# Macaron block: the attention's token sum once per sequence in the projection's bank, added to x1 by GpSimd, identity by a scaled x1

## The chip, the core and the metric

The kernel runs on one core of one Trainium2 chip. The metric is the device time in microseconds, the median of three runs. The engines are TensorE (PE; its weight loads are PEld), VectorE (DVE), ScalarE (ACT), GpSimd (POOL) and SyncE (SP), which issues every DMA. Each works through its own instruction queue in order, and they meet only through semaphores.

## The reference, cut to what matters

There are 32 sequences of 512 tokens with 256 values each, and three residual stages per sequence:

```
x = x + 0.5 * ffn(layernorm(x))      # x1
x = x + attn(layernorm(x))           # x2
x = x + 0.5 * ffn(layernorm(x))      # x3

attn(x):  a = softmax(q k^T / 16)          # 512 x 512
          a = eye + a
          a = a - mean(a, axis=-1)
          return a @ x
ffn(x):   fp4 quantise x;  g = x Wg^T, u = x Wu^T;  h = silu(g) * u
          fp4 quantise h;  return h Wd^T
```

A row of the softmax sums to 1, so a row of `eye + a` sums to 2 and its mean is 2/512. Subtracting the mean therefore subtracts 2/512 times the sum of all the tokens, the same for every row, and the identity adds the token itself. So with n = layernorm(x1), x2 = x1 + n + softmax @ n - (2/512) * sum over tokens of n.

## The kernel before, in words

The work is cut into **tiles** of 128 tokens: four tiles per sequence for the first feed-forward stage and four for the second, 256 tiles in all. Time is cut into **slots**; eight slots (j = 0 to 7) make one **iteration**, and each slot starts one tile. Slots 0 to 3 of an iteration start the first stage's tiles of sequence `it`, slots 4 to 7 the second stage's tiles of sequence `it - 2`. Besides a tile, a slot may start one of three other items: a `query` (half of a sequence's attention, two token tiles; slots 0 and 2), a `front` (layernorm and quantisation of one sequence for a feed-forward stage; slots 0 and 4), and an `afront` (layernorm and projection for the attention; slot 6). An item's steps are spread over later slots by **age**: `s.tile[2]` is the tile that was started two slots ago.

Every engine has a function `emit(s, pair)` that lists its steps of one slot in a fixed order written out by hand; `walk` runs it over the slots (two iterations form the body of a hardware loop). What one engine's slot 5 does at the same time as another's slot 5 is settled by the semaphores alone: an engine may run ahead or behind by a slot or more.

The steps of a tile n and who does them, with lines of the profile: gate and up products in three column cuts into `gu_ps` (PE, L1163 `products`); `silu` of the gate half (ACT, L851); `hid` = up * silu (DVE, L959); block maxima, scale and reciprocal `h_am`, `h_s`, `h_rs` (DVE, L971, L1014, L1045, L1076); division by the block scale `h_xq` (POOL, L586); `h_unit`, `h_sigma`, `h_sh` (ACT, L676, L679, L701); lifting `h_y` (ACT, L706); rounding `h_t`, `h_q` (DVE, L1033, L1063); dequantised halves `h_dq` (DVE, L1082 and L980); transposition `hT` by DMA (SP); the down product into `out_ps` (PE, L1264); the residual addition (DVE, L990). A gate/up product of tile n + 1 waits until ACT and DVE have read tile n out of `gu_ps`, which exists once.

The steps of an `afront`: sums, means and squares of x1 (ACT, L714, L789, L804, L831), `a_ve`, `a_rstd`, `a_shift` (POOL, L571, L599, L604), the normalised tokens `a_xs` (ACT, L796, L823), their f16 halves `xs_hi` (ACT, L845) and `xs_lo` (POOL, L593), transposition to `aT` (SP), two projections into the one bank `tr_a` (PE), read out by ACT (L818, L663). The bank's users take it in turns that are counted in `A_TURNS`; `OUT_TURNS` counts the turns of the two banks of `out_ps`.

The steps of a `query`: two score products, softmax with `s_nmax` (DVE, L941) and two exponentials (ACT, L720, L738), p in two f16 halves, `pT` by DMA, and two `attend` products into `out_ps`, each added to x1 by DVE (L1069, L951) to give x2. One `attend` is 20 matmuls of 256 columns: 12 for softmax @ n, and 8 for the identity and the mean, where a constant 128 x 128 matrix (`own_sp` for the tile's own tokens, `other_sp` for the others) multiplies the halves of all four token tiles.

The exponential and the silu use different function tables of ScalarE, so each pair of exponentials costs two table loads.

Of the kernel before, what the change touches and what calls it, by code (L numbers as in the profile page):

```python
# [159 lines left out]
def macaron_kernel(nc, x_in, wq_in, bq_in, wk_in, bk_in, wg_in, wu_in, wd_in, out):  # L160
    slots, info = schedule()
    turn_q0, turn_q1, turn_down, turn_att0, turn_att1 = (
        info[k] for k in ("q0", "q1", "down", "att0", "att1"))
    TPP, QPP, FPP, SPP = 2 * SLOTS, 2 * QPS, 4, 2
    TURNS_A = 2 * SPP
# [5 lines left out]
    with ctx:  # L171
# [36 lines left out]
        own_sp = sb("own_sp", [P, P], F16)  # L208
# [51 lines left out]
        a_shift = sb("a_shift", [P, TILES])  # L260
        a_xs = sb("a_xs", [P, TILES, D])
        xs_hi = sb("xs_hi", [P, TILES, D], F16)
# [24 lines left out]
        w_rs = sb("w_rs", [P, WCOLS // FP4_BLOCK])  # L287
# [80 lines left out]
        a_xs_done = sig("a_xs_done", 2 * TILES)  # L368
        xs_lo_done = sig("xs_lo_done", 2)
# [82 lines left out]
        def out_bank(turn):  # L452
            return out_ps[:, turn % 2, 0:D]
# [5 lines left out]
        def _(sp):  # L459
# [42 lines left out]
            def emit(s, pair):  # L502
                if s.front[1] is not None:
                    f = s.front[1]
                    sp.wait_ge(f_dl_done.sem, f_dl_done.at(f + 1, pair))
                    sp.sem_inc(sp_passed.sem, 1)
                    if pair is not None or f >= 2:
                        sp.wait_ge(gu_full.sem, gu_full.at(3 * TILES * (f - 1), pair))
                        sp.sem_inc(sp_passed.sem, 1)
                    sp.dma_start_transpose(xT[:, f % 2, :, :, :, :].rearrange("p h t c k -> p (h t c) k"),  # L510
                                           f_dq[:, :, :].rearrange("p h d -> p (h d)")).then_inc(xT_in[f % 2].sem, 16)
                if s.afront[0] is not None:
                    turn_tokens(s.afront[0], 0, pair)
                if s.query[2] is not None:
                    turn_probs(s.query[2], 0, pair)
                if s.j == 0 and 1 <= s.it + 1 < SEQS:
                    b = s.it + 1
                    at = b if pair is None else pair * 2 + b
                    if b >= 2:
                        last = [n for n, (ffn, seq, t) in enumerate(info["tile"]) if (ffn, seq, t) == (1, b - 2, TILES - 1)][0]  # L520
                        sp.wait_ge(out_added.sem, out_added.at(turn_down[last] + 1, pair))
                    sp.dma_start(x0[:, b % 2, :, :], x_view[at] if pair is None else
                                 x_view[bass.ds(at, 1)].rearrange("s p t d -> (s p) t d")).then_inc(x_loaded[b % 2].sem, 16)
                if s.query[2] is not None:
                    turn_probs(s.query[2], 1, pair)
                if s.afront[0] is not None:
                    turn_tokens(s.afront[0], 1, pair)
                if s.tile[0] is not None:
# [6 lines left out]
                    sp.dma_start_transpose(hT[:, n % 2, :, :], h_dq[:, n % 2, :]).then_inc(hT_in[n % 2].sem, 16)  # L535
                if s.j == 3 and 0 <= s.it - 3 < SEQS:
# [3 lines left out]
                    sp.wait_ge(out_added.sem, out_added.at(turn_down[last] + 1, pair))  # L540
                    sp.dma_start(out_view[at] if pair is None else
                                 out_view[bass.ds(at, 1)].rearrange("s p t d -> (s p) t d"),
                                 x3[:, b % 2, :, :]).then_inc(stored[b % 2].sem, 16)

# [6 lines left out]
        def _(pool):  # L551
            g = nc.gpsimd

            def emit(s, pair):
                if s.front[2] is not None:
                    f = s.front[2]
                    pool.wait_ge(f_ss_done.sem, f_ss_done.at(TILES * (f + 1), pair))
                    pool.sem_inc(pool_passed.sem, 1)
                    g.tensor_scalar(f_ve[:, :], f_ss[:, :], 1.0 / D, EPS, ALU.mult, ALU.add).then_inc(f_ve_done.sem, 1)
                if s.front[3] is not None:  # L560
                    f = s.front[3]
# [774 lines left out]
```

## Time and profile before

| | us |
|---|---|
| median of three runs (2389.05 to 2400.36) | 2394.25 |
| the profiled execution, its own time | 2397.43 |
| the span of the profiled execution | 2395.6 |
| PE busy (matmuls, ends modelled) | 2099.0 (88%) |
| DVE busy | 2069.8 (86%) |
| ACT busy | 1674.6 (70%) |
| POOL busy | 750.7 (31%) |
| mean granted TensorE clock | 0.969 of 2.4 GHz |

The first 73 us of the span load and quantise the weights and bring up the first tile; about 216 to 2240 us is the steady state, in which all items overlap; the last 150 us drain the pipeline. Busy times in the profile run from start to end of an instruction, and neighbours on one engine overlap by some tens of nanoseconds, so the distance from one start to the next (called pitch in the prediction) is a little shorter than the duration that is listed.

### The profile page before, as it was taken

The page shows a single profiled execution, that of the slowest core. Times are in us where ns is not written, and L with a number is a line of the kernel's source. Part 1 is how long each engine was busy: PE and PEld are TensorE (multiplying, and loading weights), DVE is VectorE, ACT ScalarE, POOL GpSimd, SP SyncE. Part 2 cuts the span into 40 slices and gives each one's busy share as a digit, 9 for nine tenths or more (in the row PEclk, how much of TensorE's full clock was granted, in tenths as well). Part 3 has the DMA queues.
Part 4 walks back from the last instruction along what each step waited for, and adds up shares of the span by engine and source line. Part 5 has one row for each costly group of instructions (what it writes and reads, how often), then busy time and mean ns, then how long its engine had stood idle before and what let it go on. Part 6 is the DMA issues. An engine that isn't in the chain of part 4 may idle for free. (4 is left out here: it accounts for less than half of the span.)

```text
span 2395.6 us, 46422 instructions
## 1 busy us (share of the span) xinstructions
PE 2099.0 (88%) x13514; PEld 1249.1 (52%) x13514; DVE 2069.8 (86%) x3961; ACT 1674.6 (70%) x4315; POOL 750.7 (31%) x664
## 2 busy tenths in 40 slices
PE   2678999999999998999989999898999999899875
PEld 1344555555555555555555555555555555555442
DVE  6567998999989898998999899898989989899764
ACT  3357777777777777777777777786777778777641
POOL 3122333332333333233333332333333233333211
PEclk9879999999999999999999999999999999999887
DMA  1233554554445445444544544445454444544432
GB/s 55 42 69 72 93 104 82 101 100 94 95 87 104 94 97 96 95 96 81 109 93 91 96 101 99 91 91 104 91 95 101 95 89 88 103 95 87 90 57 57
DMA packets 741596, 214.25 MB, mean 89 GB/s; under 512 B 706464, under 2 KB 741152, under 8 KB 741408
## 3 DMA queue, kind: packets, MB, share of 16 engines
q1 hardware_dynamic: 741408, 212.54, 45.1%
q14 instruction: 167, 1.37, 0.2%
q8 instruction: 21, 0.34, 0.1%
HBM read 19.53 MB, written 16.78 MB: 15 GB/s over the span
## 5 line engine op out<-in xcount | busy, mean ns | idle before, releaser
L1163 PE MATMUL gu_ps<-wgu_hi,xT 128*128 128x512 f16 (+1 forms) x3072 | 956.9, 366 | 64.5 <-DMA xT<-f_dq 55.0
L586 POOL TENSOR_TENSOR tile_area<-tile_area,h_rs 128x704 f32<-128x704 f32 x256 | 390.3, 1525 | 1291.1 <-DVE h_rs L1076 1291.1
L1163 PE MATMUL gu_ps<-wgu_lo,xT 128*128 128x512 f16 (+1 forms) x1536 | 562.5, 366 | 0.0
L1163 PEld LDWEIGHTS gu_ps<-wgu_hi,xT 128*128 128x128 f16 x3072 | 303.6, 99 | 377.0 <-issue 63.2
L1264 PE MATMUL out_ps<-wd_hi,hT 128*128 128x256 f16 x1536 | 364.0, 280 | 134.8 <-DMA hT<-h_dq 134.8
L1264 PE MATMUL out_ps<-wd_lo,hT 128*128 128x256 f16 (+1 forms) x1536 | 378.4, 281 | 0.0
L959 DVE SCALAR_TENSOR_TENSOR tile_area<-gu_ps,gu_unit,tile_area 128x704 f32<-128x704 f32 x256 | 241.5, 944 | 130.1 <-PE gu_ps L1163 63.7
L851 ACT ACTIVATE tile_area<-gu_ps,gu_unit 128x704 f32<-128x704 f32 x256 | 215.5, 842 | 188.8 <-PE gu_ps L1163 188.4
L706 ACT ACTIVATE h_y<-tile_area 128x704 bf16<-128x704 f32 x256 | 200.3, 782 | 92.2 <-POOL tile_area L586 92.2
L1264 PEld LDWEIGHTS out_ps<-wd_hi,hT 128*128 128x128 f16 x1536 | 153.4, 100 | 203.0 <-issue 120.3
L971 DVE TENSOR_REDUCE h_am<-tile_area 128x44 f32<-128x704 f32 x256 | 227.1, 887 | 6.7
L1033 DVE SCALAR_TENSOR_TENSOR tile_area<-h_y,tile_area 128x704 f32<-128x704 bf16 x256 | 226.4, 885 | 4.8 <-ACT h_y L706 4.8
L1063 DVE SCALAR_TENSOR_TENSOR h_q<-h_y,tile_area 128x704 f16<-128x704 bf16 x256 | 227.5, 889 | 0.2
L1163 PEld LDWEIGHTS gu_ps<-wgu_lo,xT 128*128 128x128 f16 x1536 | 152.0, 99 | 125.1 <-issue 7.1
L1264 PEld LDWEIGHTS out_ps<-wd_lo,hT 128*128 128x128 f16 (+1 forms) x1536 | 151.9, 99 | 82.4 <-issue 57.0
L1163 PE MATMUL out_ps<-xs_hi,pT 128*128 128x256 f16 x1024 | 191.0, 275 | 3.0 <-DMA pT<-p 3.0
L1264 PE MATMUL out_ps<-wd_late,hT 128*128 128x256 f16 x1280 | 192.5, 283 | 0.0
L676 ACT ACTIVATE h_unit<-h_rs 128x1 f32<-128x1 f32 x256 | 49.8, 195 | 179.4 <-DVE h_rs L1076 175.9
L1163 PE MATMUL sc_ps<-aT,qT_hi 128*128 128x512 f16 x512 | 154.0, 383 | 2.4 <-DVE p L999 1.2
L565 POOL TENSOR_TENSOR f_xq<-f_xn,f_rs 128x1024 f32<-128x1024 f32 x64 | 124.0, 1937 | 93.1 <-DVE f_rs L937 93.1
L980 DVE TENSOR_TENSOR h_dq<-h_q,h_sl 128x704 f16<-128x704 f16 x256 | 144.2, 563 | 0.0
L1163 PE MATMUL out_ps<-xs_lo,pT 128*128 128x256 f16 x512 | 140.8, 275 | 0.0
(169 smaller groups left out, 4090.7 us busy)
## 6 DMA issues: line engine op xcount, KB each, us to landing
x<-in_L_attn_x SPq DMA_DIRECT2D x32, 512.0 KB, 3.9
out<-x_later SPq DMA_DIRECT2D x32, 512.0 KB, 3.6
hT<-h_dq SPq DMA_TRANSPOSE x256, 3.6
pT<-p SPq DMA_TRANSPOSE x128, 3.2
xT<-f_dq SPq DMA_TRANSPOSE x64, 4.3
w_raw<-in_L_ffn_w_down SPq DMA_DIRECT2D x1, 704.0 KB, 7.5
w_raw<-in_L_ffn_w_gate SPq DMA_DIRECT2D x1, 640.0 KB, 4.6
w_raw<-in_L_ffn_w_up SPq DMA_DIRECT2D x1, 640.0 KB, 5.7
```

The lines of the kernel that those rows point to most:

```text
L565: g.tensor_tensor(blocks(f_xq[:, :], XB), blocks(f_xn[:, :], XB), per_block(f_rs[:, :], XB), ALU.mult).then_inc(f_xq_done.sem, 1)
L586: g.tensor_tensor(blocks(h_xq[:, n % 2, :], FB), blocks(hid[:, n % 2, :], FB), per_block(h_rs[:, n % 2, 0:FB], FB), ALU.mult).then_inc(xq_ ...
L676: a_.activation(h_unit[:, n % 2:n % 2 + 1], h_rs[:, n % 2, FB:FB + 1], ACT.Copy, scale=-SH).then_inc(unit_done.sem, 1)
L706: a_.activation(h_y[:, n % 2, :], h_xq[:, n % 2, :], ACT.Abs, scale=LIFT).then_inc(lifted.sem, 1)
L851: a_.activation(sg[:, n % 2, :], gu_ps[:, 0:FF], ACT.Silu, scale=gu_unit[:, :]).then_inc(silu_done.sem, 1)
L959: v.scalar_tensor_tensor(out=hid[:, n % 2, :], in0=gu_ps[:, FF:GU], scalar=gu_unit[:, :], in1=sg[:, n % 2, :], op0=ALU.mult, op1=ALU.mult) ...
L971: v.tensor_reduce(h_am[:, n % 2, 0:FB], blocks(hid[:, n % 2, :], FB), AX.X, ALU.max, apply_absolute_value=True).then_inc(am_done.sem, 1)
L980: v.tensor_tensor(pairs(h_dq[:, n % 2, FF:2 * FF]), pairs(h_q[:, n % 2, :]), per_pair(h_sl[:, n % 2, :, :], FB), ALU.mult).then_inc(dl_don ...
L1033: v.scalar_tensor_tensor(out=h_t[:, n % 2, :], in0=h_y[:, n % 2, :], scalar=ROUND_MIN, in1=h_xq[:, n % 2, :], op0=ALU.max, op1=ALU.add).th ...
L1063: v.scalar_tensor_tensor(out=h_q[:, n % 2, :], in0=h_y[:, n % 2, :], scalar=ROUND_MIN, in1=h_t[:, n % 2, :], op0=ALU.max, op1=ALU.subtract ...
L1163: ins = t_.matmul(dst, x, y, start=(i == 0), stop=(i == len(todo) - 1))
L1264: ins = t_.matmul(out_bank(turn_down[n]), h, w, start=(i == 0), stop=(i == len(terms) - 1))
```

## The change

1. `attend` keeps its 12 matmuls of softmax @ n; the 8 matmuls with constants are gone, and so is `own_sp`. A new product `add_tokens`, once per sequence, forms the same 8 products with `other_sp` (minus 2/512 times the sum of the tokens) in the bank `tr_a`, as a third turn after the two projections.
2. ScalarE reads that out to `token_sum` (128 x 256), and scales x1 in place, tile by tile: x1 = x1 * (1 + a_rstd / SX) + a_shift / SX, which is x1 + n. The factors `a_own` come from two small GpSimd instructions.
3. GpSimd adds `token_sum` to the four tiles of x1 in one instruction of 128 x 1024 values.
4. VectorE's two additions that give x2 are the same instructions; each waits for `x1_ready` (and for the previous reader of x2) as well.
5. The order of the steps of a slot is written anew on all five queues, and most steps are one or two slots older. The tile's steps, before to after: first two cuts of gate/up on PE 0 to 1, third cut 0 to 2, silu 0 to 2, `hid` and block maxima 0 to 1, the rest up to `h_rs` 0 to 2, GpSimd's `h_xq` 2 to 3, ScalarE's `h_sh`, `h_y` 2 to 4, rounding 1 to 3, low half of `h_dq` 2 to 3, down product 3 to 5, addition 3 to 5; SyncE's `hT` stays at 0. A query's scores go from 2 to 3 (first) and 4 (second), its exponentials from 3 to 5, its attends from 5 to 6 and 7. The projections go from age 3 to 4 and 5, the token sum has age 6. On SyncE the transposition of a `front` goes from the head of the slot's list to behind `hT`, and the two of an `afront` go together ahead of the query's.
6. `w_rs` lies in `a_xs` during the setup (memory only). Waits on `out_added` for two tiles take the later of two turns.

The diff, cut to its core, in the order turns, TensorE, GpSimd, ScalarE, VectorE. The ScalarE step that is shown for t = 0, 1 stands a second time, for t = 2, 3, at `afront[7]`; the VectorE step stands at `query[6]` and `query[7]`.

```diff
-A_TURNS = (("q0", "afront", 3), ("q1", "afront", 3))
-OUT_TURNS = (("att0", "query", 5), ("att1", "query", 5), ("down", "tile", 3))
+A_TURNS = (("q1", "afront", 5), ("sum", "afront", 6), ("q0", "afront", 4))
+OUT_TURNS = (("down", "tile", 5), ("att0", "query", 6), ("att1", "query", 7))
...
             def attend(a, i, turn):
-                t = 2 * (a % QPS) + i
                 return products(out_bank(turn), [(pT[:, i, 0, k, :], pT[:, i, 1, k, :], xs_hi[:, k, :], xs_lo[:, k, :])
-                                                 for k in range(TILES)],
-                                [((own_sp if k == t else other_sp)[:, :], xs[:, k, :])
-                                 for k in range(TILES) for xs in (xs_hi, xs_lo)])
+                                                 for k in range(TILES)])
+            def add_tokens():
+                return products(tr_a[:, 0:D], [], [(other_sp[:, :], xs[:, k, :]) for k in range(TILES) for xs in (xs_hi, xs_lo)])
...
+                if s.afront[6] is not None:
+                    b = s.afront[6]
+                    pe.wait_ge(xs_hi_done.sem, xs_hi_done.at(b + 1, pair))
+                    pe.wait_ge(xs_lo_done.sem, xs_lo_done.at(b + 1, pair))
+                    if pair is not None or turn_sum[b] >= 1:
+                        pe.wait_ge(a_free.sem, a_free.at(turn_sum[b], pair))
+                    add_tokens().then_inc(a_full.sem, 1)
...
+                    g.tensor_scalar(a_own[:, 0:TILES], a_rstd[:, :], 1.0 / SX, 1.0, ALU.mult, ALU.add).then_inc(a_own_done.sem, 1)
+                    g.tensor_scalar(a_own[:, TILES:2 * TILES], a_shift[:, :], 1.0 / SX, 0.0, ALU.mult, ALU.add).then_inc(a_own_done.sem, 1)
+                    pool.wait_ge(xs_hi_done.sem, xs_hi_done.at(b + 1, pair))
...
+                    g.tensor_tensor(xs_lo[:, :, :], a_xs[:, :, :], xs_hi[:, :, :], ALU.subtract).then_inc(xs_lo_done.sem, 1)
...
-                if s.tile[2] is not None:
-                    n = s.tile[2]
+                if s.tile[3] is not None:
+                    n = s.tile[3]
                     pool.wait_ge(rs_done.sem, rs_done.at(n + 1, pair))
...
+                if s.afront[7] is not None:
+                    b = s.afront[7]
+                    pool.wait_ge(a_free.sem, a_free.at(turn_sum[b] + 1, pair))
+                    pool.wait_ge(x1_own_done.sem, x1_own_done.at(TILES * (b + 1), pair))
+                    g.tensor_tensor(x1[:, b % 2, :, :], x1[:, b % 2, :, :],
+                                    token_sum[:, :].unsqueeze(1).broadcast_to([P, TILES, D]), ALU.add).then_inc(x1_ready.sem, 1)
...
+                if s.afront[5] is not None:
+                    b = s.afront[5]
+                    act.wait_ge(a_own_done.sem, a_own_done.at(2 * b + 2, pair))
+                    act.wait_ge(a_xs_done.sem, a_xs_done.at(TILES * b + 2, pair))
+                    for t in (0, 1):
+                        a_.activation(x1[:, b % 2, t, :], x1[:, b % 2, t, :], ACT.Identity, scale=a_own[:, t:t + 1],
+                                      bias=a_own[:, TILES + t:TILES + t + 1]).then_inc(x1_own_done.sem, 1)
...
+                if s.afront[7] is not None:
+                    b = s.afront[7]
+                    act.wait_ge(a_full.sem, a_full.at(turn_sum[b] + 1, pair))
+                    if pair is not None or b >= 1:
+                        act.wait_ge(x1_ready.sem, x1_ready.at(b, pair))
+                    a_.activation(token_sum[:, :], tr_a[:, 0:D], ACT.Copy, scale=1.0 / (SP * SX)).then_inc(a_free.sem, 1)
...
                     dve.wait_ge(out_full.sem, out_full.at(turn_att1[a] + 1, pair))
+                    dve.wait_ge(x1_ready.sem, x1_ready.at(seq + 1, pair))
+                    if pair is not None or seq >= 2:
+                        dve.wait_ge(f_xn_done.sem, f_xn_done.at(TILES * (front_of[(2, seq)] + 1 - FPP), pair))
                     v.scalar_tensor_tensor(out=x2[:, seq % 2, t, :], in0=out_bank(turn_att1[a]), scalar=1.0 / (SP * SX),
                                            in1=x1[:, seq % 2, t, :], op0=ALU.mult, op1=ALU.add).then_inc(out_added.sem, 1)
```

After the change the order of a tile's steps in VectorE's slot is: addition (age 5), `h_am` total (2), `h_t` and `h_sl` (3), `h_q` (3), `h_s` (2), high `h_dq` (3), `h_rs` (2), low `h_dq` (3), `hid` (1), block maxima (1). ScalarE's slot 2 reads, in order: `h_unit`, `h_sigma`, `h_sh`, `h_y` (age 4), `a_xs` (four), `xs_hi`, sums of a front's tiles 2 and 3, their mean, squares of its tiles 0 and 1, silu (age 2). GpSimd's slot 2 reads: `a_rstd`, `a_shift`, `a_own` (two), `xs_lo`, `h_xq`; `a_ve` is the last step of its slot 1.

## Rows read from the trace of the kernel before

**Rows 1.** Busy (count) PE, PEld, DVE, ACT, POOL; clock, DMA share, GB/s.

```profile
1201.00:1547.00 346.00, 317.54 (x2097) 190.17 (x2096) 315.74 (x609) 258.16 (x670) 113.80 (x101) 1.00 0.48 95
```

**Rows 2.** Timeline of VectorE (start us, us): one step, twice, four iterations apart.

```profile
1237.00 1.03 DVE L976 TENSOR_TENSOR qT_lo<-qT,qT_hi 128x512 f16<-128x512 f32 x1
...
1513.71 1.03 DVE L976 TENSOR_TENSOR qT_lo<-qT,qT_hi 128x512 f16<-128x512 f32 x1
```

**Rows 3.** Waits of VectorE, same stretch: us, times, longest; largest and last.

```profile
DVE tile_area L959 <- ACT tile_area L851: 10.3, 6, 2.7
DVE tile_area L959 <- PE gu_ps L1163: 3.6, 5, 0.7
...
DVE x_later L990 <- PE out_ps L1264: 0.8, 1, 0.8
```

**Rows 4.** Waits of TensorE in the same stretch, the two largest.

```profile
PE out_ps L1264 <- DMA hT<-h_dq: 15.4, 13, 2.3
PE tr_a L1163 <- DMA aT<-xs_lo: 8.6, 5, 2.1
```

**Rows 5.** Timeline of VectorE: a slot with tile work alone, and the next `hid`.

```profile
1218.09 0.95 DVE L959 SCALAR_TENSOR_TENSOR tile_area<-gu_ps,gu_unit,tile_area 128x704 f32<-128x704 f32 x1
...
1227.15 0.95 DVE L959 SCALAR_TENSOR_TENSOR tile_area<-gu_ps,gu_unit,tile_area 128x704 f32<-128x704 f32 x1 [2.58 <-ACT tile_area L851]
```

**Rows 6.** Timeline of ScalarE in the same slot, ahead of that late `hid`.

```profile
1220.85 0.20 ACT L697 ACTIVATE f_nm<-f_sum 128x2 f32<-128x2 f32 x1 [1.86 <-issue]
...
1221.90 0.40 ACT L751 ACTIVATE f_scrap<-x_later 128x256 f16<-128x256 f32 x1
...
1222.69 1.07 ACT L796 ACTIVATE a_xs<-x_later,a_shift,a_rstd 128x256 f32<-128x256 f32 x2
...
1224.87 1.06 ACT L845 ACTIVATE xs_hi<-a_xs 128x1024 f16<-128x1024 f32 x1
1225.83 0.83 ACT L851 ACTIVATE tile_area<-gu_ps,gu_unit 128x704 f32<-128x704 f32 x1
1226.56 0.49 ACT L866 ACTIVATE f_scrap<-x_later,f_nm 128x256 f16<-128x256 f32 x1
...
1227.54 0.49 ACT L872 ACTIVATE f_scrap<-x_later,f_nm 128x256 f16<-128x256 f32 x1
```

**Rows 7.** Timeline of TensorE: an attend's first matmul, and the one behind its 20th.

```profile
1214.73 0.27 PE L1163 MATMUL out_ps<-xs_hi,pT 128*128 128x256 f16 x1
...
1216.91 0.33 PE L1163 MATMUL gu_ps<-wgu_hi,xT 128*128 128x384 f16 x1
```

**Rows 8.** Instruction groups by form over the span: busy us, mean ns.

```profile
L796 ACT ACTIVATE a_xs<-x_later,a_shift,a_rstd 128x256 f32<-128x256 f32 x64 | 34.5, 586 | 1.8 <-POOL a_shift L604 1.8
...
L892 ACT ACTIVATE wd_late<-sc_ps,w_scale 128x256 f16<-128x256 f32 x2 | 0.9, 466 | 0.0
...
L980 DVE TENSOR_TENSOR h_dq<-h_q,h_sl 128x704 f16<-128x704 f16 x256 | 144.2, 563 | 0.0
...
L565 POOL TENSOR_TENSOR f_xq<-f_xn,f_rs 128x1024 f32<-128x1024 f32 x64 | 124.0, 1937 | 93.1 <-DVE f_rs L937 93.1
```

**Rows 9.** Timeline of GpSimd: a tile's `h_xq` and the attention's norm.

```profile
1217.59 1.45 POOL L586 TENSOR_TENSOR tile_area<-tile_area,h_rs 128x704 f32<-128x704 f32 x1 [0.77 <-DVE h_rs L1076]
...
1220.24 0.21 POOL L604 TENSOR_TENSOR a_shift<-a_nm,a_rstd 128x4 f32<-128x4 f32 x1 [0.23 <-POOL a_rstd L599]
```

**Rows 10.** Timelines of GpSimd and VectorE: `xs_lo`, and an `h_dq` that starts under it.

```profile
1294.77 2.13 POOL L593 TENSOR_TENSOR xs_lo<-a_xs,xs_hi 128x1024 f16<-128x1024 f32 x1
...
1296.40 0.88 DVE L980 TENSOR_TENSOR h_dq<-h_q,h_sl 128x704 f16<-128x704 f16 x1
```

**Rows 11.** Timelines of GpSimd and TensorE at the head: last weights, first two tiles.

```profile
53.50 1.49 POOL L632 TENSOR_TENSOR w_raw<-tile_area,w_s 128x768 f32<-128x768 f32 x1 [3.42 <-DVE tile_area L1118]
...
67.33 0.59 PE L1163 MATMUL gu_ps<-wgu_hi,xT 128*128 128x512 f16 x1 [17.27 <-DMA xT<-f_dq]
...
79.81 0.58 PE L1163 MATMUL gu_ps<-wgu_hi,xT 128*128 128x512 f16 x1 [0.66 <-issue]
```

More of the change, by code:

```diff
@@ L717, in emit @@
+                if s.query[5] is not None:
+                    a = s.query[5]
                     act.wait_ge(bias_done.sem, bias_done.at(a + 1, pair))
@@ L760, in emit @@
+                if s.front[3] is not None:
+                    f = s.front[3]
                     ffn, seq = info["front"][f]
@@ L984, in emit @@
+                if s.tile[5] is not None:
+                    n = s.tile[5]
                     ffn, seq, t = info["tile"][n]
@@ new lines, in emit @@
+                if s.tile[3] is not None:
+                    n = s.tile[3]
+                    dve.wait_ge(lifted.sem, lifted.at(n + 1, pair))
+                    v.scalar_tensor_tensor(out=h_t[:, n % 2, :], in0=h_y[:, n % 2, :], scalar=ROUND_MIN,
+                                           in1=h_xq[:, n % 2, :], op0=ALU.max, op1=ALU.add).then_inc(t_done.sem, 1)
+                    dve.wait_ge(sh_done.sem, sh_done.at(n + 1, pair))
+                    v.scalar_tensor_tensor(out=h_sl[:, n % 2, :, :], in0=twice(h_s[:, n % 2, 0:FB], FB),
+                                           scalar=h_unit[:, n % 2:n % 2 + 1], in1=h_sh[:, n % 2, :, :],
+                                           op0=ALU.mult, op1=ALU.subtract).then_inc(sl_done.sem, 1)
@@ new lines, in emit @@
+                if s.front[3] is not None:
+                    f = s.front[3]
+                    dve.wait_ge(f_lifted.sem, f_lifted.at(f + 1, pair))
+                    v.scalar_tensor_tensor(out=f_t[:, :], in0=f_y[:, :], scalar=ROUND_MIN, in1=f_xq[:, :],
+                                           op0=ALU.max, op1=ALU.add).then_inc(f_t_done.sem, 1)
+                if s.tile[3] is not None:
+                    n = s.tile[3]
+                    dve.wait_ge(t_done.sem, t_done.at(n + 1, pair))
+                    v.scalar_tensor_tensor(out=h_q[:, n % 2, :], in0=h_y[:, n % 2, :], scalar=ROUND_MIN,
+                                           in1=h_t[:, n % 2, :], op0=ALU.max, op1=ALU.subtract).then_inc(q_done.sem, 1)
@@ L995, in emit @@
+                if s.query[4] is not None:
+                    a = s.query[4]
                     dve.wait_ge(scale_done.sem, scale_done.at(a + 1, pair))
@@ L1071, in emit @@
[L1071 to L1083 removed]
+                    dve.wait_ge(hid_done.sem, hid_done.at(n + 1, pair))
```

841 lines of the change are left out of this document (415 added, 426 removed).

## The prediction

> **What bounds the kernel now.** I read first the busy table of a steady stretch, then the waits of the two busiest engines there, then the timelines around the longest wait. In the stretch of 346.0 us TensorE is busy for 317.5 us, VectorE for 315.7, ScalarE for 258.2 and GpSimd for 113.8 [rows 1]: two engines at 91 to 92% and none full. The stretch holds five iterations, since a step that occurs once per iteration lies (1513.71 - 1237.00) / 4 = 69.2 us apart [rows 2]. VectorE's waits come in nine rows of together 26.6 us, of which the first two and the last are shown [rows 3], 5.3 per iteration, so its work alone is 69.2 - 5.3 = 63.9 us. TensorE's come in four rows of together 28.3 us, of which the two largest are shown [rows 4], 5.7 per iteration, all but 0.7 of the 28.3 for a DMA; its work is 63.5 us. Either engine would allow an iteration of about 64 us, and the other 5 us are a matter of who waits for whom.
>
> VectorE is the end that counts, because the longest waits sit there: `hid` behind the silu, 10.3 of the 26.6 us [rows 3]. The timeline shows one. VectorE starts `hid` of a slot that holds tile work and one attention addition alone at 1218.09 and has nothing left 6.5 us later; the next `hid` comes 2.58 us late, released by ScalarE [rows 5]. ScalarE meanwhile had sat 1.86 us at a step for which the profile names no releaser, and then went through sums, `a_xs`, `xs_hi` before the silu at 1225.83 [rows 6]. So the worst wait is ScalarE's list in a light slot of VectorE, not a matmul.
>
> **Part 1, the matmuls that go.** An attend of 20 matmuls takes 1216.91 - 1214.73 = 2.18 us, 0.109 each [rows 7]. A sequence has four attends; 32 constant matmuls go and 8 come back, so TensorE loses 24 x 0.109 = 2.6 us per iteration, 84 us in all, and has 60.9 us of work left. VectorE loses nothing: its two additions stay. Its 63.9 us are therefore the floor of the iteration, and the removed matmuls are worth at most the 5.3 us of waits, and only those that TensorE causes.
>
> **Part 2, the work that comes.** ScalarE gets four scalings of x1, the form of `a_xs` at 0.586 us, and one read of 128 x 256 from PSUM, 0.47 by `wd_late` [rows 8]: 2.8 us per iteration at most, 54.4 in place of 51.6. GpSimd gets two small instructions of about the 0.21 us of `a_shift` [rows 9] and the addition of 1024 columns, between `f_xq`'s 1.94 [rows 8] and `xs_lo`'s 2.13 [rows 10]: 2.4 to 2.6 us on an engine that is a third busy. None is a bound by its sum; what counts is whom they hold up. The scalings wait for `a_own` and for `a_xs`, both a slot old. GpSimd's addition stands behind `h_xq` in its slot 5, and VectorE's first reader behind `h_rs` in its slot 6, about 8 us later for 2 us of work, so `x1_ready` costs nothing; were it late, low `h_dq` and `hid` would stand behind it. TensorE's token sum waits for ScalarE's second projection read, with the next gate/up queued behind, but that waits for a silu that comes later in ScalarE's list anyway. On SyncE `xT` goes behind `hT` and the two `aT` ahead of `pT`; the low `h_dq` that starts `hT` now stands ahead of `hid` in VectorE's list instead of behind the block maxima, some 2 us earlier, and this covers most of the hT wait of 15.4 / 5 = 3.1 us per iteration [rows 4].
>
> **Part 3, the order.** I follow the new lists of all engines through one iteration with the starts of the timelines, from VectorE's `h_rs` in slot 0 until that step comes round again. Most slots close without a wait, because TensorE's load is now even: before, slots 5 and 7 carried two attends each, 4.4 us on top of a tile; after, slots 6, 7, 0 and 1 carry one each of 12 x 0.109 = 1.3 us, and TensorE's work per slot is 60.9 / 8 = 7.6 us on average against VectorE's 8.0. Waits appear in five places.
> Slot 1: `hid` needs the silu at the end of ScalarE's slot 2. From `h_rs` the chain is: `h_xq` to `a_shift` end 1220.45 - 1217.59 = 2.9 us [rows 9], with `a_ve` between them now, 0.4 more, 3.3; four `a_xs` 1224.87 - 1222.69 = 2.2; `xs_hi` 1.0; sums of two tiles 1222.69 - 1221.90 = 0.8; their mean 0.2; two squares 1227.54 - 1226.56 = 1.0; silu 0.7 to 0.8 [rows 6]: together 9.3 us. VectorE gets from `h_rs` to this `hid` in one light slot, 6.5 us [rows 5], and one low `h_dq`, 0.4 net of overlap: 6.9. Wait 2.4 us.
> Slot 0: the silu stands behind x1's sums and squares, which wait for the addition: 0.3. Slot 2: `h_xq` stands behind `xs_lo`, which waits for `xs_hi`, so `h_t` comes 0.2 late, and `f_xn` comes 0.3 late. Slot 3: the addition behind the projection, 0.2.
> Sum 3.4 us. The iteration becomes 63.9 + 3.4 = 67.3, which is 1.9 less. The gap of 1.86 us in ScalarE [rows 6] then falls into a slot 0 in which the silu is ready some 3.5 us before VectorE asks for it, by the same walk.
>
> A cost from both sides: GpSimd's new addition may slow a VectorE step beside it. The low `h_dq` takes 0.88 us under `xs_lo` [rows 10] against 0.56 on average [rows 8]; one such meeting per iteration costs 0.3 us, none costs 0, and no row speaks for a gain. I take 0, since the VectorE steps that stand beside the addition are not the two halves of `h_dq`; 0.3 x 29 = 9 us more stay in the range.
> The Trainium skill (Perfetto Trace Analysis, Optimizing Scalar/DVE Operations) says that GpSimd and VectorE share a read port, so that moving work between them might not help. By that rule the iteration would be 67.6 in place of 67.3; the row of 0.88 us agrees in kind.
>
> **Head and tail.** At the head the first layernorm's GpSimd steps move behind the last weight unit, which ends at 54.99 [rows 11]; I put the first gate/up 5 us later than 67.33. But TensorE's remaining weight transposes, which lie between the first tile and the second at 79.81 [rows 11], now come ahead of the first tile, while it would wait anyway. Net -2 us, within 6 either way. The tail has the same chain from the last `hid` to the store: 0, within 6.
>
> **Sum.** The steady state, 216 to 2240 us, holds 29 iterations: 29 x 1.9 = 55 us, and 2 at the head. The profiled execution took 2397.4 us, so it becomes 2340; it stood 3.2 above the median 2394.25, so I predict 2337 us. Its own bounds: waits of 2.0 to 4.7 us per iteration give 2298 to 2375.
>
> **Rivals.**
> *Waits nearly vanish* (0.2). If ScalarE reaches its slot 2 earlier than I have it, the 2.4 us go and the waits are 0 to 1.5 us: 29 x 3.8 to 5.3 gives 2238 to 2282. For it: TensorE and the DMAs have slack everywhere. Against: `h_unit` pins ScalarE's list to `h_rs`.
> *No gain* (0.14). VectorE's work is what it was, and waits of 5.3 us come back in other places: 2392. For it: the longest wait of before was ScalarE's, and ScalarE gets more work.
> The Trainium skill (Perfetto Trace Analysis, Identifying the Most-Contended Engine) says that matmul busy time misleads because matmuls are pipelined, and that for VectorE occupancy is a fair measure. By that rule VectorE is the bound and the change does not relieve it; the waits above say that it is not full.
> *ScalarE becomes the pacemaker, slower* (0.12). The scalings stand ahead of `h_y` in slot 5 and ahead of `f_xn` in slot 3, the token sum ahead of a silu. If all 2.7 us land in front of VectorE, the iteration is 67.3 + 2.7 = 70.0: 29 x 0.8 = 23 us more, 2415. It decides from 1.9 us on. For it: table loads share slot 5. Against: I find `hid` in slots 3 to 5 ready 1 us or more ahead of VectorE.
> *TensorE's clock falls, the change brings less work but not less time* (0.04). It was granted 1.00 in the stretch [rows 1] with waits of up to 2.3 us [rows 4]; I see one idle of 2.8 us in slot 2. If one tile's gate/up ran at 1.2 instead of 2.4 GHz, 3.5 us more, the 6.4 us of TensorE's room would take it; two would bring back 2390.
>
> **Chances.** Forecast 0.5, rivals 0.2, 0.14, 0.12, 0.04. About 0.5% (12 us) is what a measurement of this kernel can tell from no change. Faster: the forecast but for its upper edge and the first rival, 0.70. Same: 0.17. Slower: 0.13. The range that leaves out 2 in 10 reaches from 2250, inside the first rival, to 2404, short of the slower one.
>
> **What would show it.** In the profile after: attends of 12 matmuls, 1.3 us; VectorE busy as before, its waits down to some 3.4 us per iteration with the largest still `hid` behind the silu, in the slot in which ScalarE does `a_xs`; TensorE's wait for hT mostly gone; `x1_ready` in no row of waits; an iteration of 67.3 us. Wrong if `hid` waits for TensorE, if VectorE's longest wait is for a scaling or `x1_ready`, or if its work per iteration is not 63.9 us.

## The result and the profile after

The changed kernel takes 2376.1 us (median of 6 runs, 2369.2 to 2380.0) against 2395.0 for the kernel before: a ratio of 0.992, with a 95% interval of 0.990 to 0.994. That is 0.8% faster; forecast were 2337 us, 2.4%. The profiled execution took 2375.2 us with a span of 2372.8.

The busy row of the same stretch of 346 us after the change, columns as in [rows 1]:

```profile
1200.00:1546.00 346.00, 312.52 (x1955) 181.22 (x1956) 323.92 (x604) 269.85 (x692) 125.86 (x115) 0.96 0.48 95
```

VectorE is busy for 323.9 us instead of 315.7, ScalarE for 269.9 instead of 258.2, and TensorE's granted clock is no longer 1.00. VectorE's timeline with the step that [rows 2] show, in four of its five places:

```profile
1228.66 0.68 DVE L984 TENSOR_TENSOR qT_lo<-qT,qT_hi 128x512 f16<-128x512 f32 x1
...
1295.57 0.68 DVE L984 TENSOR_TENSOR qT_lo<-qT,qT_hi 128x512 f16<-128x512 f32 x1
...
1367.76 0.68 DVE L984 TENSOR_TENSOR qT_lo<-qT,qT_hi 128x512 f16<-128x512 f32 x1
...
1508.47 0.68 DVE L984 TENSOR_TENSOR qT_lo<-qT,qT_hi 128x512 f16<-128x512 f32 x1
```

Four iterations take 279.8 us, 70.0 each, no less than the 69.2 of before. But they alternate: 66.9 us, then 72.2 (over the whole loop 67.5 and 72.0 on average). From the first such step to the last of the 32 the two kernels take 2134.5 and 2133.8 us, so the steady state gained nothing; 6.1 us of the 22.8 in the spans lie ahead of it and 16.0 behind it.

VectorE's waits in the stretch (us, times, longest), the answer to [rows 3], and two of TensorE's, the answer to [rows 4]:

```profile
DVE f_dq L961 <- issue: 9.3, 3, 3.2
DVE s_nmax L1087 <- PE sc_ps L1205: 5.3, 3, 1.8
DVE f_am L1073 <- ACT f_xn L831: 1.4, 5, 0.3
DVE tile_area L1111 <- ACT tile_area L908: 0.8, 5, 0.2
DVE p L1119 <- ACT p L685: 0.5, 2, 0.3
```

```profile
PE sc_ps L1205 <- ACT rho L894: 7.5, 5, 1.5
...
PE out_ps L1259 <- DMA hT<-h_dq: 1.0, 2, 0.5
```

The wait of `hid` for the silu is gone (0.8 after 10.3), and so is TensorE's for hT (1.0 after 15.4). In their place stand a gap of 3 us for which the profile names no releaser, and a wait for the scores. The gap lies in the longer iterations; the wait lies in these and in one of the shorter, the one from 1367.76, which takes 68.6 us. The timelines of VectorE and TensorE where one begins, and the busy row of the 5 us behind it:

```profile
1200.13 0.89 DVE L1124 TENSOR_REDUCE h_am<-tile_area 128x44 f32<-128x704 f32 x1
1204.20 0.69 DVE L961 TENSOR_TENSOR f_dq<-f_q,f_sh 128x1024 f16<-128x1024 f16 x1 [3.19 <-issue]
```

```profile
1205.94 0.40 PE L1259 MATMUL out_ps<-wd_hi,hT 128*128 128x256 f16 x1 [3.35 <-DVE x_later L974]
1206.13 0.42 PE L1259 MATMUL out_ps<-wd_lo,hT 128*128 128x256 f16 x1
```

```profile
1206.00:1211.00 5.00, 5.00 (x23) 3.18 (x24) 4.97 (x9) 4.87 (x18) 1.77 (x3) 0.50 0.56 105
```

`f_dq` is the first step in the body of VectorE's loop, and the gap occurs 13 times over the span, once between two runs of the loop's body, which is gone through 14 times: VectorE stands while the loop turns. TensorE, which needs a buffer of out_ps from it, idles 3.35 us, and in the 5 us behind that its granted clock is 0.50, the lower of its two levels (1.2 GHz): one matmul of 256 columns follows the other after 0.21 us instead of 0.11.

### The profile page after: what moved, and what is told of

The parts are those of the page before. It is cut to its first block, busy times and chain, and to the rows that moved or that the text cites. A ratio compares the mean times of both kernels' runs of the same rounds, so it can differ in the third digit from the quotient of the medians.

```text
span 2372.8 us, 45698 instructions
## 1 busy us (share of the span) xinstructions
PE 2049.9 (86%) x12746; PEld 1184.7 (50%) x12746; DVE 2135.3 (90%) x3961; ACT 1752.3 (74%) x4475; POOL 831.4 (35%) x759
## 4 chain that ended last, share of the span: by engine, by line
issue 60%; POOL 15%; DVE 10%; ACT 10%; PE 3%; DMA 1%; POOLq 1%; DVEq 0%; ACTq 0%; SPq 0%
POOL tile_area L612 6%; POOL x_later L618 3%; POOL f_rstd L589 2%; POOL a_rstd L564 1%; ACT a_xs L755 1%; DVE tile_area L1009 1%; ACT xs_hi L793 1%; ACT a_xs L774 1%; PE out_ps L1259 1%; PE gu_ps L1205 1%; DVE f_t L1018 1%; DVE tile_area L1111 1%; ACT L908 1%; ACT L762 1%; ACT f_xn L785 1%
## 5 line engine op out<-in xcount | busy, mean ns | idle before, releaser
L1205 PE MATMUL gu_ps<-wgu_hi,xT 128*128 128x512 f16 (+1 forms) x3072 | 929.4, 364 | 87.1 <-ACT tile_area L908 41.6
L612 POOL TENSOR_TENSOR tile_area<-tile_area,h_rs 128x704 f32<-128x704 f32 x256 | 381.9, 1492 | 1229.9 <-DVE h_rs L1060 1229.9
L1259 PE MATMUL out_ps<-wd_hi,hT 128*128 128x256 f16 x1536 | 370.2, 283 | 86.8 <-DMA hT<-h_dq 45.0
L1259 PE MATMUL out_ps<-wd_lo,hT 128*128 128x256 f16 (+1 forms) x1536 | 384.4, 284 | 0.0
L1205 PE MATMUL sc_ps<-aT,qT_hi 128*128 128x512 f16 x512 | 172.2, 421 | 47.7 <-ACT rho L894 43.0
L1078 DVE TENSOR_TENSOR h_dq<-h_q,h_sl 128x704 f16<-128x704 f16 x256 | 213.3, 833 | 0.0
L1205 PE MATMUL out_ps<-xs_hi,pT 128*128 128x256 f16 x1024 | 197.5, 281 | 9.6 <-DVE x_later L1068 8.8
```

What stands on the lines that cost most here:

```text
L612: g.tensor_tensor(blocks(h_xq[:, n % 2, :], FB), blocks(hid[:, n % 2, :], FB), per_block(h_rs[:, n % 2, 0:FB], FB), ALU.mult).then_inc(xq_ ...
L1078: v.tensor_tensor(pairs(h_dq[:, n % 2, FF:2 * FF]), pairs(h_q[:, n % 2, :]), per_pair(h_sl[:, n % 2, :, :], FB), ALU.mult).then_inc(dl_don ...
L1205: ins = t_.matmul(dst, x, y, start=(i == 0), stop=(i == len(todo) - 1))
L1259: ins = t_.matmul(out_bank(turn_down[n]), h, w, start=(i == 0), stop=(i == len(terms) - 1))
```

## The experiments

Three theories for the missing gain. *Turn*: the loop's jump has become dearer. *Port*: VectorE's low `h_dq` is held while GpSimd works, since its mean rose from the 563 ns of [rows 8] to 833, 69 us over the span (the group by form in the changed kernel stands below). *Load* (formed once the parts had been run alone): the load of x comes late, and TensorE's scores behind it.

```profile
L1078 DVE TENSOR_TENSOR h_dq<-h_q,h_sl 128x704 f16<-128x704 f16 x256 | 213.3, 833 | 0.0
```

**The loop written out, in both kernels.**

```
-    with engine.Fori(0, PAIRS) as pair:
-        for s in slots:
-            if LOOP_FROM <= s.it < LOOP_FROM + 2:
-                emit(s, pair)
+    for s in slots:
+        emit(s, None)
```

> The changed kernel with the loop over pairs of iterations written out, so that no engine jumps back; every other instruction and its order as in the changed kernel. Turn theory: in the changed kernel the iterations with a loop turn are 72.2 us apart and those without 67.0, because VectorE stands about 3.2 us in front of f_dq at the turn and TensorE works at its lower clock right after; without the 14 turns all iterations take about 67: 2376 - 14 x 5.2 = 2303 us (2295 to 2320), and VectorE's row f_dq behind issue (39.3 us) is gone. Port theory (the gain is eaten by the low h_dq, which is held under GpSimd's h_xq in slots 0 and 1): the alternation has another cause, the time stays at 2370 to 2380. A third way: the instructions of a written-out program have to be fetched all the time and the gaps come everywhere, over 2380.

> The kernel before with the loop over pairs written out, nothing else. Turn theory: before, the alternation is 69.8 against 68.1 us, since its gap falls on ScalarE in a slot in which VectorE has most of it covered; 14 x 1.7 to 2.3 go: 2394 - 24 to 32 = 2362 to 2370. Then the change is worth 2365 - 2303 = some 60 us where no loop turns, which is what was forecast for the looped one. Port theory: no change, 2390 to 2395.

Measured: 2314.4 us (2311.4 to 2318.3) and 2352.3 (2347.6 to 2353.5). So the loop costs 61.8 us after the change, 4.4 for each of 14 turns, and 42.7 before, 3.1 for each. The alternation and VectorE's row of `f_dq` behind issue are gone, so fetching a written-out program costs it nothing that shows. Without turns the change is worth 38 us, twice what it shows, but not 60: the kernel before gained more than I expected, since its iterations without a turn became shorter too (68.3 us on average in the loop). Written out, its iterations are 67.7 us on average, not 69.2; those of the changed kernel are 67.3.

**Four iterations per turn.**

```
-PAIRS = (LOOP_TO - LOOP_FROM) // 2
+PAIRS = (LOOP_TO - LOOP_FROM) // 4
-            if LOOP_FROM <= s.it < LOOP_FROM + 2:
+            if LOOP_FROM <= s.it < LOOP_FROM + 4:
...
```

The lines left out give the semaphore counts and the addresses of x and of the output their step of four iterations.

> The changed kernel with four iterations in the loop's body instead of two, so 7 turns instead of 14. Turn theory: half of the turns' price goes, 7 x 5.2 = 36 us: 2340 us (2330 to 2350). Port theory: 2370 to 2380.

Measured: 2349.3 us (2341.6 to 2352.6). Seven turns fewer give 27 us, 3.8 each: the turn theory again. Part of the difference to 4.4 can be no turn: the loop also costs something in every iteration, as the load's runs below show.

**Low `h_dq` ahead of `h_rs`.**

```
+                    v.tensor_tensor(pairs(h_dq[:, n % 2, FF:2 * FF]), pairs(h_q[:, n % 2, :]),
+                                    per_pair(h_sl[:, n % 2, :, :], FB), ALU.mult).then_inc(dl_done.sem, 1)
...
                     v.reciprocal(h_rs[:, n % 2, :], h_s[:, n % 2, :]).then_inc(rs_done.sem, 1)
...
-                    v.tensor_tensor(pairs(h_dq[:, n % 2, FF:2 * FF]), pairs(h_q[:, n % 2, :]),
-                                    per_pair(h_sl[:, n % 2, :, :], FB), ALU.mult).then_inc(dl_done.sem, 1)
```

> The changed kernel with one step of VectorE's list moved: the low h_dq stands directly ahead of h_rs instead of behind it, so GpSimd's h_xq, which h_rs releases, can no longer run beside it. Port theory: the low h_dq takes 0.46 us in all slots instead of 1.7 and 2.3 in slots 0 and 1, VectorE has 3.1 us less work per iteration: up to 69 + 30 us less, 2280 to 2310. Turn theory: in slot 1 the time only turns back into the wait of hid for the silu, in slot 0 some 1 us goes: 10 to 35 us less, 2340 to 2366, and h_rs, 0.4 us later, takes part of it back.

Measured: 2384.2 us (2383.0 to 2385.2), 8 slower, outside what either theory expected. Low `h_dq` takes 523 ns on average and VectorE's busy time is 2064.0 us instead of 2135.3, but this row stands among its waits in the stretch of 1200 to 1546:

```profile
DVE tile_area L1111 <- ACT tile_area L908: 15.3, 8, 3.8
```

The time in which VectorE was held has turned back into the wait of `hid` for the silu, and `h_rs`, now later, starts the chain to that silu later too. The port theory falls as a cause of time here.

**The turn at another slot.**

```
-LOOP_FROM, LOOP_TO = 3, SEQS - 1
+LOOP_FROM, LOOP_TO = 3, SEQS - 3
+TURN = 1
...
-            if LOOP_FROM <= s.it < LOOP_FROM + 2:
+            if (LOOP_FROM, TURN) <= (s.it, s.j) < (LOOP_FROM + 2, TURN):
...
```

> The changed kernel with the loop's body beginning at slot 1 of an iteration instead of slot 0 (and 13 turns instead of 14); the order of every engine's work is untouched. If a turn costs VectorE its 3.0 us wherever it lies, because VectorE has no wait left to cover it: 2376 less one turn of 4.4 us = 2372 us (2365 to 2380), with the gap in front of the first step of slot 1. If the price is that of its place in front of f_dq: the gap moves to another engine, as in the kernel before, where it stood in front of ScalarE, and 13 x 1.4 us go (3.1 per turn before against 4.4 after): 2350 to 2358.

Measured: 2376.4 us (2371.4 to 2379.9). VectorE's gap has moved to the first step of slot 1, with 3.1 us each, as before it stood in front of `f_dq`:

```profile
DVE x_later L975 <- issue: 37.2, 12, 3.2
```

With 13 turns in place of 14, 4 us less would have been the same price per turn; within the spread, the slot makes no difference.

**The parts alone, without turns.** All three runs have the loop written out. In the kernel before:

```
-                                [((own_sp if k == t else other_sp)[:, :], xs[:, k, :])
-                                 for k in range(TILES) for xs in (xs_hi, xs_lo)])
```

> The kernel before with the loop written out and attends of 12 matmuls: the 8 constant matmuls of each attend, and with them the identity and the mean, are left out and nothing takes their place. It prices the removed matmuls alone, in the old order, against 2352 us for the same kernel with them. VectorE as the floor: TensorE loses 3.5 us per iteration, but VectorE waits only some 2.5 us per iteration for TensorE, half of which may go: 2315 to 2345. If the matmuls paced the kernel: 30 x 3.5 = 105 less, 2250. If they are hidden: 2352.

In the changed kernel:

```
+                                [(other_sp[:, :], xs[:, k, :]) for k in range(TILES) for xs in (xs_hi, xs_lo)])
```

> The changed kernel with the loop written out and 8 constant matmuls put back into each attend (the sum over tokens is added to the attention's output once more, so the output differs by it). It prices the matmuls in the new order, against 2314 us without them. VectorE as the floor, with 66 us of work per iteration: TensorE has 60.9 + 3.5 = 64.4, under the 66, so at most 0.5 per iteration, 2314 to 2330. If the removed matmuls are what the change gains: 2352 and more.

```
-                    g.tensor_tensor(x1[:, b % 2, :, :], x1[:, b % 2, :, :],
-                                    token_sum[:, :].unsqueeze(1).broadcast_to([P, TILES, D]), ALU.add).then_inc(x1_ready.sem, 1)
+                    g.tensor_tensor(x1[:, b % 2, :, 0:8], x1[:, b % 2, :, 0:8],
+                                    token_sum[:, 0:8].unsqueeze(1).broadcast_to([P, TILES, 8]), ALU.add).then_inc(x1_ready.sem, 1)
...
-                        a_.activation(x1[:, b % 2, t, :], x1[:, b % 2, t, :], ACT.Identity, scale=a_own[:, t:t + 1],
+                        a_.activation(x1[:, b % 2, t, 0:8], x1[:, b % 2, t, 0:8], ACT.Identity, scale=a_own[:, t:t + 1],
...
-                    a_.activation(token_sum[:, :], tr_a[:, 0:D], ACT.Copy, scale=1.0 / (SP * SX)).then_inc(a_free.sem, 1)
+                    a_.activation(token_sum[:, 0:8], tr_a[:, 0:8], ACT.Copy, scale=1.0 / (SP * SX)).then_inc(a_free.sem, 1)
```

> The changed kernel with the loop written out and the work that came with the change shrunk: the four scalings of x1, the read of the token sum and GpSimd's addition take 8 columns of each 256 (so identity and mean are missing in the other columns); their waits and their places stay. Against 2314 us. If that work is hidden, as forecast: 2310 to 2316. If ScalarE's 1.7 us or GpSimd's 2 us stand in VectorE's way: up to 30 x 1.7 = 50 less, 2264 to 2300.

Measured: 2294.3, 2326.4 and 2305.2 us. In the old order the removed matmuls alone are worth 58 us, more than I allowed them; that kernel, which forms neither identity nor mean, takes 20 us less than the changed one without turns. In the new order the same matmuls cost 12. The work that came costs 9, between the two expectations (the four times spread from 2299.6 to 2311.8). The 58 us are for 32 matmuls per sequence, of which the change brings 8 back: taken in proportion, 24 of them and the new work would bring 58 x 24/32 - 9 = some 34 us in the old order, where the change without turns brings 38. Whether the new order as such gives or takes is not shown by these prices. The changed kernel without turns and the one with little new work show the same wait, of `s_nmax` for the scores. Its origin, in the timelines of the changed kernel without turns (SyncE, ScalarE, TensorE, VectorE):

```profile
1256.57 7.37 SPq L520 DMA_TRANSPOSE hT<-h_dq  x2
1263.98 0.91 SPq L506 DMA_DIRECT2D x<-in_L_attn_x  x1
```

```profile
1269.70 0.42 ACT L866 ACTIVATE f_scrap<-x 128x256 f16<-128x256 f32 x1 [3.39 <-DMA x<-in_L_attn_x]
...
1270.51 0.34 ACT L886 ACTIVATE rho<-sc_ps,beta,rho_unit 128x4 f32<-128x4 f32 x1
```

```profile
1270.95 0.71 PE L1197 MATMUL sc_ps<-aT,qT_hi 128*128 128x512 f16 x2 [2.79 <-issue]
1271.45 0.63 PE L1197 MATMUL sc_ps<-aT,qT_lo 128*128 128x512 f16 x1
```

```profile
1275.43 1.22 DVE L1079 TENSOR_REDUCE s_nmax<-sc_ps 128x2 f32<-128x1024 f32 x1 [3.06 <-PE sc_ps L1197]
```

SyncE issues the load of x only at 1263.98, behind two transposes to hT. ScalarE's sums of x wait 3.39 us for it, with `rho` next in ScalarE's list. TensorE idles 2.79 us and starts 0.10 us behind the end of `rho` (no releaser is named here; in the looped kernel's row above it is `rho`), and then runs the scores at its lower clock, one matmul of 512 columns every 0.43 us instead of 0.22, and VectorE waits 3.06 us for them. In the kernel before, the same load was issued 10.8 us ahead of the step that reads it, in the changed kernel 5.7 (1263.98 to 1269.70):

```profile
1240.74 0.39 SPq L522 DMA_DIRECT2D x<-in_L_attn_x  x1
```

```profile
1251.58 0.41 ACT L657 ACTIVATE f_scrap<-x 128x256 f16<-128x256 f32 x1
```

The load has not moved in SyncE's list: in both kernels it is the first step of slot 0, behind the transposition to hT of slot 7. That transposition waits for the low `h_dq`, whose age the change raised from 2 to 3, while the first sums of x stayed at age 0 of their `front`.

**The load earlier, without and with turns, and the held step moved.** The load of x (the first and third runs have the loop written out; the looped one has 13 turns, LOOP_TO being SEQS - 3):

```
-                if s.j == 0 and 1 <= s.it + 1 < SEQS:
-                    b = s.it + 1
+                if s.j == 5 and 1 <= s.it + 2 < SEQS:
+                    b = s.it + 2
```

> The changed kernel with the loop written out and the load of x issued three slots earlier in SyncE's list; nothing else. Load theory: in the new order the load stands behind two transposes to hT, ScalarE's sums wait 2.3 us for it (63 us in 28 waits), rho stands behind them, TensorE idles 2.8 us for rho and then runs the scores at its lower clock, and VectorE's s_nmax waits for these (48 us in 26 waits). With the load early all of that goes: 2314 - 30 to 45 = 2269 to 2284 us, iterations of 66.0 us throughout. If rho or the scores are late for another reason: 2305 to 2316.

> The changed kernel with its loop (13 turns instead of 14) and the load of x three slots earlier. Load theory: iterations without a turn 66.0 instead of 66.7 to 68.7; in those with a turn VectorE's 3.0 us stay, and TensorE still falls to its lower clock behind them: 2376 - 4 - 25 to 40 = 2332 to 2347. If the turn alone makes the waits of s_nmax: 2365 to 2376.

On top of the first of these, in VectorE's list:

```
-                if s.tile[3] is not None:
+                if s.tile[3] is not None and s.j not in (0, 1):
...
                                            in1=sg[:, n % 2, :], op0=ALU.mult, op1=ALU.mult).then_inc(hid_done.sem, 1)
+                if s.tile[3] is not None and s.j in (0, 1):
+                    n = s.tile[3]
+                    dve.wait_ge(sl_done.sem, sl_done.at(n + 1, pair))
+                    v.tensor_tensor(pairs(h_dq[:, n % 2, FF:2 * FF]), pairs(h_q[:, n % 2, :]),
+                                    per_pair(h_sl[:, n % 2, :, :], FB), ALU.mult).then_inc(dl_done.sem, 1)
```

> As the run with the early load and the loop written out, and in slots 0 and 1 VectorE's low h_dq stands behind hid instead of ahead of it, so that GpSimd's h_xq and xs_lo hold it for a shorter time. Chain theory (in slots 0 and 1 the steps of ScalarE and GpSimd from h_rs to the silu set the time, and the held h_dq only fills a wait): within 8 us of the run with the early load. Port theory (the 2.1 us per iteration that VectorE is held are what is missing): 30 to 60 us less than it.

Measured: 2274.6 us (2272.5 to 2277.6), 2341.8 (2339.8 to 2343.3) and 2280.6 (2276.9 to 2283.2). The load theory holds with its number: 39.7 us without turns, most iterations 65.9 to 66.0 us, one row left among VectorE's waits in the stretch of 1200 to 1546, and the granted clock there is 1.00:

```profile
DVE f_am L1065 <- ACT f_xn L823: 1.4, 5, 0.3
```

```profile
1200.00:1546.00 346.00, 320.91 (x2095) 189.75 (x2094) 341.00 (x641) 282.83 (x727) 132.45 (x119) 1.00 0.53 101
```

VectorE looks full, 341.0 of 346. The third run shows that it is not. With low `h_dq` behind `hid` in two slots VectorE's busy time falls by 84 us, to 2035.4, the kernel is 6 us slower, and a wait takes the place of the busy time (the profile names no releaser for most of it):

```profile
DVE tile_area L1103 <- issue: 13.5, 9, 2.3
DVE tile_area L1103 <- ACT tile_area L900: 2.3, 1, 2.3
```

In slots 0 and 1 the chain through GpSimd and ScalarE to the silu sets the time, and the held step only fills the wait. VectorE's timeline shows both waits of one iteration:

```profile
1227.81 0.95 DVE L1103 SCALAR_TENSOR_TENSOR tile_area<-gu_ps,gu_unit,tile_area 128x704 f32<-128x704 f32 x1 [0.87 <-issue]
...
1235.83 0.95 DVE L1103 SCALAR_TENSOR_TENSOR tile_area<-gu_ps,gu_unit,tile_area 128x704 f32<-128x704 f32 x1 [2.29 <-issue]
```

ScalarE's silu starts at 1226.88 and 1234.90 and takes 0.83 us each time, so `hid` starts 0.10 us behind its end in both slots:

```profile
1226.88 0.83 ACT L900 ACTIVATE tile_area<-gu_ps,gu_unit 128x704 f32<-128x704 f32 x1
...
1234.90 0.83 ACT L900 ACTIVATE tile_area<-gu_ps,gu_unit 128x704 f32<-128x704 f32 x1
```

The looped run (the second) shows a cost of the loop besides its turns. I had expected 66.0 us for an iteration without a turn; inside the loop most take 66.7, and one behind the loop 65.95, with the same instructions. In one such iteration VectorE has small gaps of about 0.1 us ahead of several steps (0.13 us ahead of `s_mneg`, for example, instead of 0.04). Writing the loop out removes this too, so the prices per turn above hold more than the jump.

The run with the early load and no turns is the fastest of all: 0.9495 of the kernel before, interval 0.9479 to 0.9511.

**The place of VectorE's jump.** VectorE's slot is divided into a part up to `hid` (`emit_early`) and the rest with `hid` and its block maxima (`emit_hid`), and the body of its loop begins between them; in the kernel before, where a slot begins with `hid`, the division lies behind the block maxima:

```
+                emit_early(at[LOOP_FROM, 0], None)
+                with dve.Fori(0, PAIRS) as pair:
+                    for s, then in zip(body, body[1:] + [at[LOOP_FROM + 2, 0]]):
+                        emit_hid(s, pair)
+                        emit_early(then, pair)
```

> The changed kernel with its loop, and the body of VectorE's loop alone begins ahead of hid, where it began in the kernel before, instead of behind the block maxima of hid; the order of its work is untouched. If the place at which VectorE jumps decides whether it stands (as 0 in the kernel before against 3.0 us per turn in the changed one): the gap goes, 14 x 3 to 4.4 us: 2314 to 2335. If any jump of VectorE costs it 3 us now: 2370 to 2380, with the gap in front of hid.

> The kernel before with its loop, and the body of VectorE's loop alone begins behind the block maxima of hid, where it begins in the changed kernel; the order of its work is untouched. Place theory (a jump of VectorE behind the block maxima costs it 3.0 us, one ahead of hid at most 1.0): VectorE now stands some 3 us at each of 14 turns, 2395 + 20 to 42 = 2415 to 2437 us. If the kernel before is free of the gap for another reason: 2390 to 2400.

Measured: 2350.2 us (2342.5 to 2354.0) and 2412.2 (2410.6 to 2414.5). The first lies between its two expectations: VectorE's gap shrinks from 3.0 to 1.0 us, and ScalarE now stands 13.9 us in 13 gaps ahead of `s_scale`, where it stood 3.4 in 11; in the second run the kernel before, which had none on VectorE, gets one of 2.2 and is 17 us slower, just short of the 20 to 42 expected. The rows of the two over their spans:

```profile
DVE tile_area L1113 <- issue: 11.5, 12, 1.0
```

```profile
DVE h_dq L982 <- issue: 28.7, 13, 2.3
```

The same instructions in the same order, cut at two places: the place decides a good part of a turn's price. The answer for the changed kernel's DMA from 1198 to 1206, around one gap, has a row of instruction transfers:

```profile
q14 instruction: 3, 0.02, 1.0%
```

The trace has the start of each. At each of the 38 gaps in the changed kernel and in these two runs a transfer of 8 KB starts 1.9 to 2.3 us before VectorE goes on. It starts 0.9 to 1.0 us after VectorE has run out of work in the changed kernel, 0.2 to 0.4 after in the kernel before with its jump moved, and 1.1 to 1.2 before it has run out in the changed kernel with its jump moved; the gaps of 3.0, 2.2 and 1.0 us differ by that. This agrees with VectorE waiting for its next instructions; that the transfers are VectorE's own, and why they start sooner at one place than at another, the traces do not show.

**Both together.** The early load and this cut in the looped kernel, with 13 turns:

> The changed kernel with its loop (13 turns), the early load of x, and VectorE's body beginning ahead of hid. If the two causes add: 2342 - 13 x 1.9 (what the cut gave per turn without the early load) = 2317 us (2308 to 2325). If the cut only helped because VectorE had the waits of the late load to cover the jump: 2335 to 2345.

Measured: 2331.9 us (2326.3 to 2333.3), between the two expectations: the cut gives 10 us on top of the early load, after 26 without it. VectorE's gap is gone but for one of 1.0, but iterations with a turn still take 2.9 us more; among VectorE's waits stands `hid` for gate/up, 1.9 us per turn, and ScalarE stands 14.9 us in 12 gaps ahead of `s_scale`. Whether the rest of the turn's price lies in the other engines' jumps was not tested.

## Why the prediction was half right

*The account.* Without turns and with the load early the change brings 2352.3 - 2274.6 = 77.7 us. The late load takes 39.7 of this back (2314.35 - 2274.64), the dearer loop 61.8 - 42.7 = 19.1. That 18.9 are left, as measured, is no check: the terms are differences of the same five times. Nor do they add in any order: in the looped kernel the early load brings 2376.1 - 2341.8 = 34.3 us, with a turn less, and with the load early the loop costs 2341.8 - 2274.6 = 67.2, 5.2 for each of 13 turns.

*Bound and floor.* Right that neither TensorE nor VectorE was full. The iteration of 69.2 us [rows 2] was read as a schedule's, though it held 1.5 us of the loop; the iterations of before alternate by 2 us, and that was in the trace. The sum of the new order's waits was right, its parts roughly: with the held step out of the way, an iteration of 66.1 us has 3.4 us of them (2.29 in slot 1, 0.87 in slot 0 and about 0.3 for `f_xn`, where 2.4, 0.3 and 0.3 were forecast, and 0.4 elsewhere), and VectorE's work is 62.7 us, not 63.9. That the changed kernel without turns takes the 67.3 us that were forecast is luck: the work is 1.2 less, and the late load adds 1.3 that the sum did not hold.

*Part 1.* Right in size: an attend takes 1.31 us now (1196.58 to 1197.89 in TensorE's timeline), and TensorE's busy time falls by 2075.0 - 1996.3 = 79 us from the kernel before without turns to the changed one without turns and with the early load (84 forecast). The 58 us that all 32 matmuls are worth in the old order, 2.0 per iteration of 29, are no more than the 2.1 us per iteration that VectorE waited for TensorE (10.6 of the 26.6 in the rows of [rows 3] and those left out there).

*Part 2.* Right that the new work is nearly hidden (9 us by the shrunk run), that `x1_ready` stands in no row of waits, and that hT's wait goes. The step that failed is the one on SyncE: I followed `xT`, `hT`, `aT` and `pT` past each other and left out the load of x, which shares that queue and comes behind a transposition to hT that now waits a slot longer. It was worth 39.7 us without turns, the largest part of the miss.

*Part 3, slot 1.* The chain of 9.3 us to the silu was right: with `h_dq` out of the way it takes 9.0, from `h_xq` at 1226.75 to the silu's end at 1235.73. The wait of 2.4, reckoned with low `h_dq` ahead of it, is 2.3 without; in the changed kernel it appears as busy time. Low `h_dq` starts under GpSimd's `xs_lo` and ends when that ends (timelines of GpSimd and VectorE, changed kernel without turns):

```profile
1252.72 2.27 POOL L593 TENSOR_TENSOR xs_lo<-a_xs,xs_hi 128x1024 f16<-128x1024 f32 x1 [2.72 <-ACT xs_hi L785]
```

```profile
1253.28 2.10 DVE L1070 TENSOR_TENSOR h_dq<-h_q,h_sl 128x704 f16<-128x704 f16 x1
1255.49 0.95 DVE L1103 SCALAR_TENSOR_TENSOR tile_area<-gu_ps,gu_unit,tile_area 128x704 f32<-128x704 f32 x1
```

2.10 us, where 0.47 is its time when GpSimd is idle; my bound of 0.3 per meeting from [rows 10] was too low, since there `h_dq` had started 0.5 us ahead of the end of `xs_lo`. The Trainium skill (SBUF — State Buffer, SBUF: two separate sides) says that of a VectorE instruction with two SBUF inputs and a GpSimd instruction that reads SBUF the first to start gets the shared ports for its whole length and the other blocks. The rows agree: `h_dq` ends 0.39 us behind the end of `xs_lo`, and 0.38 behind it in [rows 10].

*Part 3, slot 0.* The sentence on ScalarE's gap of 1.86 us [rows 6] failed, the second step that did. I took it for a property of ScalarE that moves into a slot with room. It was the turn of the loop: with the loop written out that row is gone from the kernel before. In the new order VectorE stands at the turn, 3.0 us each time, where there is no room; the prediction had put nothing for it.

*Head and tail.* The first gate/up came 5.5 us later (at 72.87; 5 forecast), and the first `qT_lo` all the same 6.1 earlier (131.25 after 137.37; 2 forecast). The tail's 16 us were not forecast; 6.8 of them go in the kernel before too when its loop is written out, the rest stays unexplained.

*The rivals.* TensorE's clock did fall, which I gave 0.04. Its price was not absorbed by TensorE's room, because the slowed matmuls were scores and VectorE's next step reads them. "Waits nearly vanish" is what the changed kernel does once load and turns are out of the way: 2274.6 us, in its range of 2238 to 2282, but not by its reason, since the wait of slot 1 stays, inside the held low `h_dq`.

## What to carry to other kernels

When a queue's order is rewritten, list every transfer in it, also those that the change does not mean to touch, and compare for each the time from issue to first use before and after: here that of one load fell from 10.8 us to 5.7, 3.4 of them a wait, though the load kept its place in the list. Look whether iterations alternate before taking their mean as the schedule's, and price the turn of a hardware loop as a step of its own, on each engine. A busy row is not work: an instruction that is held by another engine counts as busy, and shortening it gives nothing where it only filled a wait.

## What the runs showed of the hardware

A loop cost 3.1 and 4.4 us per turn in two orders of one kernel; four iterations per turn instead of two saved 3.8 for each turn that went. VectorE showed no gap at its jump in the kernel before and one of 2.2 with the jump moved, 3.0 in the changed kernel and 1.0 with it moved, each pair with the same instructions in the same order; in each of these gaps VectorE went on 1.9 to 2.3 us behind the start of an instruction transfer. TensorE's granted clock fell to 0.50 behind an idle of 3.35 us, and behind one of 2.79 the scores ran at half their pace, so that VectorE, which reads them next, waited 3.06.
